# Expert stage of a fused attention and mixture-of-experts layer: hand-overs two pairs of blocks apart, TensorE's steps in reverse order, paired row loads

## The reference

```python
x = x + attention(layernorm(x))              # x: (8, 512, 256)
h = layernorm(x).reshape(4096, 256)
topv, topi = top_k(h @ gate_w.T, 8)          # 8 of 64 experts for each token
rw = softmax(topv)
gate, up = split(einsum('nh,eih->nei', h, gu_w))   # 64 + 64 columns per expert
out = einsum('nei,ehi->nh', silu(gate) * up * W, dp_w)   # W holds rw at topi, else 0
shared = (silu(h @ sh_gate_w.T) * (h @ sh_up_w.T)) @ sh_down_w.T
x = x + out + sigmoid(h @ sh_gate1_w.T) * shared
```

## Time and profile before

| | us |
|---|---|
| median of 3 runs | 1461.35 |
| lowest and highest of them | 1455.36, 1462.63 |
| the profiled execution, its own time | 1475.3 |
| its span from first to last instruction | 1473.5 |
| expert stage: first turn_x to last turn_x | 866.5 to 1425.3 |
| POOL's indirect writes: first to last issue | 876.1 to 1443.2 |
| PE, POOL busy over the whole span | 78%, 50% |

### The profile page before, as it was taken

How to read it: one execution, slowest core, us unless ns; L and a number is a source line. 1 busy time by engine, 2 the same in 40 slices (tenths; PEclk the granted TensorE clock), 3 DMA queues, 4 the chain that set the end, 5 groups by cost and what they waited for, 6 DMA issues and landing times. The chain is left out here.

```text
span 1473.5 us, 26911 instructions
## 1 busy us (share of the span) xinstructions
PE 1155.0 (78%) x7746; PEld 865.3 (59%) x7746; DVE 710.1 (48%) x2210; ACT 665.7 (45%) x1650; POOL 729.7 (50%) x978
## 2 busy tenths in 40 slices
PE   3799989898998989988874048788788888878871
PEld 2566666565665666665543047677677677667650
DVE  2566766566564665655422411111244444444455
ACT  2466555555554455543321024444444445444530
POOL 3101127556374463744556735555555555556541
PEclk9799999999898999988866569999899999999985
DMA  2687757212122121211229655555567777666534
GB/s 77 203 274 239 244 176 249 75 52 91 40 97 71 52 83 47 94 61 64 72 76 325 206 158 157 159 156 160 207 228 259 263 241 261 222 238 219 173 113 153
DMA packets 144735, 233.45 MB, mean 158 GB/s; under 512 B 19831, under 2 KB 122438, under 8 KB 139216
## 3 DMA queue, kind: packets, MB, share of 16 engines
q1 hardware_dynamic: 69776, 101.07, 21.6%
q0 software_dynamic: 27648, 69.28, 13.1%
q10 hardware_dynamic: 47168, 61.35, 12.9%
HBM read 107.32 MB, written 132.66 MB: 163 GB/s over the span
## 5 line engine op out<-in xcount | busy, mean ns | idle before, releaser
L1299 POOL DMA_INDIRECT res_d<-y,dst_i x320 | 319.8, 999 | 261.0 <-ACT y L1151 141.5
L817 DVE TENSOR_REDUCE nmax<-ps 128x1 f32<-128x512 f32 (+3 forms) x448 | 226.2, 532 | 183.2 <-PE ps L474 150.3
L424 POOL DMA_INDIRECT rows_d<-pay,slot_i x256 | 257.4, 1005 | 74.4 <-issue 70.7
L684 ACT ACTIVATE wgu_s<-ps 128x512 f32<-128x512 f32 x320 | 192.0, 601 | 198.9 <-PE ps L515 168.7
L1239 PE MATMUL psB<-wgu_s,xT 128*128 x1280 | 184.0, 290 | 34.2 <-issue 22.7
L472 PE MATMUL ps<-kT,qT 96*128 96x512 f32 (+3 forms) x512 | 198.3, 432 | 9.1 <-DVE nmax L817 6.8
L513 PE MATMUL ps<-qT,kT 128*128 128x512 f32 (+3 forms) x512 | 194.5, 424 | 3.4 <-ACT qT L697 3.2
L1239 PEld LDWEIGHTS psB<-wgu_s,xT 128*128 128x128 f32 x1280 | 166.2, 203 | 43.2 <-issue 42.7
L1066 DVE TENSOR_TENSOR inner<-inner,psB 128x128 f32<-128x128 f32 x160 | 45.6, 285 | 288.4 <-ACT inner L1138 228.4
L1257 PE MATMUL psD<-wdp_s,innerT 128*128 x640 | 178.2, 404 | 0.0
L1131 ACT COPY xT<-psA 128x512 f32<-128x512 f32 x160 | 95.2, 595 | 118.2 <-PE psA L1228 92.0
(11 more groups left out here) (194 smaller groups left out, 1696.5 us busy)
## 6 DMA issues: line engine op xcount, KB each, us to landing
rows_d<-blank ACTq DMA_DIRECT2D x8, 5440.0 KB, 18.9
xg<-rows_d SPq DMA_DIRECT2D x320, 136.0 KB
yk<-res_d SPq DMA_DIRECT2D x32, 1024.0 KB
wgu_s<-wgu_in ACTq DMA_DIRECT2D x8, 1024.0 KB
x_d<-x SPq DMA_DIRECT2D x32, 192.5 KB
xs<-x_d SPq DMA_DIRECT2D x32, 192.5 KB
res_d<-y,dst_i POOLq DMA_INDIRECT x320
wgu_s<-x_in SPq DMA_DIRECT2D x32, 128.0 KB, 2.7
```

The source lines that it names most:

```text
L424: pool.indirect_dma_start(rows_d, bass.IndirectOffsetOnAxis(ap=slot_i[par][:, t, k:k + 1], axis=0), pay[par][:, t, :], None).then_inc(s_sc ...
L684: act.activation(pexp[p % 4][:, s, :], ps2[:, (5 * p + s) % 2, :], ACT.Exp, scale=HEAD_D ** -0.5).then_inc(s_exp, 1)
L817: return dve.tensor_reduce(nmax[u][:, tile, heads[0]:heads[-1] + 1], src, AX.X, ALU.max, negate=True)
L1299: pool.indirect_dma_start(res_d, bass.IndirectOffsetOnAxis(ap=dst_i[:, j % G:j % G + 1], axis=0), y[:, j % Y, :], None, bounds_check=ROUTE ...
```

## The change

**Distances.** PE and ACT now do the four operations of pair i in steps i, i+2, i+4 and i+6 (`GATE`, `TURN`, `DOWN` = 2, 4, 6) and no longer in i to i+3. There are 167 steps instead of 164.

**Order.** Within a step both engines go from the oldest pair to the newest: down(i-6), turn_inner(i-4), gate_up(i-2), turn_x(i). Waits that this order implies are dropped.

**Buffers.** `xT`, `inner`, `innerT` get three buffers (`A`); `psC` gets two banks, and the shared expert uses their free columns instead of `psS`. `dst_i` holds 32 blocks, `y` holds 10 instead of 12.

**Loads.** SP loads two blocks with one DMA (160 of 272 KB) on one semaphore.

**Sums.** All eight additions go to `acc`; `mix` writes `fin` and comes one step after the last addition, in the sixth step of the tile (`MIX` = 5). Because it reads a bank that PE's turn_inner writes in the next step, PE waits there for `mix` (`c_mix`, named shared_added). Sums begin 12 steps after a sequence is complete instead of 9. Five tiles are late instead of four.

```diff
-            G, R, Y = 16, 4, 12
+            G, R, Y, A = 16, 4, 10, 3
+            GATE, TURN, DOWN = 2, 4, 6
-            dst_i = sb("dst_i", [P, G], I32)
+            dst_i = sb("dst_i", [P, 2 * G], I32)
-            psC = ps("psC", [P, SEQ])
-            psS = ps("psS", [P, SEQ])
+            psC = ps("psC", [P, 2, SEQ])
...
-            STEPS = PAIRS + 4
-            LOADED_BEFORE, SUMMED_AFTER, SUM_STEPS = 20, 9, 4
+            STEPS = PAIRS + DOWN + 1
+            LOADED_BEFORE, SUMMED_AFTER = 26, 12
+            SUM_STEPS, TURN_SHARED, DOWN_SHARED, MIX = 4, 2, 4, 5
...
-                    sp.dma_start(xg[:, j % G, :], rows_v[j]).then_inc(e_x[j % G], 16)
+                    sp.dma_start(xg[:, j % G:j % G + 2, :], rows_v[i]).then_inc(e_x[i % (G // 2)], 16)
...
                 def mix(tile):
-                    dve.wait_ge(c_acc[u], TOP * (tile // 2) + TOP - 1)
+                    dve.wait_ge(c_acc[u], TOP * (tile // 2 + 1))
                     dve.wait_ge(c_y_ps, tile + 1)
-                    dve.tensor_tensor(acc[:, u], psS[:, P:P + D], acc[:, u], ALU.add).then_inc(c_mix, 1)
+                    step = STEPS if tile in late_sums else sum_step(tile) + DOWN_SHARED
+                    dve.wait_ge(e_c, min(PAIRS, step - TURN + 1))
...
                 def turn_x(i):
-                    if i >= 2:
-                        pe.wait_ge(e_a, i - 1)
...
                 def gate_up(i):
                     pe.wait_ge(e_a, i + 1)
-                    if i >= 2:
-                        pe.wait_ge(e_in, i - 1)
...
                 def turn_inner(i):
                     pe.wait_ge(e_in, i + 1)
-                    if i >= 1:
-                        pe.wait_ge(e_c, i)
...
                 for i in range(STEPS):
                     if i % 2 == 0 and i < PAIRS:
                         load_offsets(2 * i)
+                    if 0 <= i - DOWN < PAIRS:
+                        down(i - DOWN)
...
+                    for tile, s in tile_at(i - 1):
+                        if s == MIX:
+                            pe.wait_ge(c_mix, tile + 1)
...
+                    if 0 <= i - TURN < PAIRS:
+                        turn_inner(i - TURN)
+                    if 0 <= i - GATE < PAIRS:
+                        gate_up(i - GATE)
                     if i < PAIRS:
                         turn_x(i)
-                    if 0 <= i - 1 < PAIRS:
-                        gate_up(i - 1)
-                    if 0 <= i - 2 < PAIRS:
-                        turn_inner(i - 2)
-                    if 0 <= i - 3 < PAIRS:
-                        down(i - 3)
```

More of the change, by code:

```diff
@@ L963, in build @@
                  "dst_ready shared_tanh shared_gate sh_ready shT_psum shT_ready shared_psum shared_added").split()]
-            e_x = [sem(f"xg_in{k}") for k in range(G)]
+            e_x = [sem(f"xg_in{k}") for k in range(G // 2)]
             e_out = [sem(f"y_out{k}") for k in range(Y)]
@@ L981, in every @@
             def every(tile):
-                return 4 if tile // TILES == BATCH - 2 else 8
+                return 6 if tile // TILES == BATCH - 2 else 8
             def load_turn(tile):
@@ L991, in sum_step @@
                 return (complete(tile) + every(tile) * (tile % TILES)) // 2 + SUMMED_AFTER
-            late_sums = [tile for tile in range(ALL_TILES) if sum_step(tile) + SUM_STEPS >= STEPS]
+            late_sums = [tile for tile in range(ALL_TILES) if sum_step(tile) + MIX >= STEPS]
             def tile_at(step):
                 return [(tile, step - sum_step(tile)) for tile in range(ALL_TILES)
-                        if tile not in late_sums and 0 <= step - sum_step(tile) < SUM_STEPS]
+                        if tile not in late_sums and 0 <= step - sum_step(tile) <= MIX]
+            shared_bank = [(sum_step(tile) if tile not in late_sums else tile) % 2 for tile in range(ALL_TILES)]
             block = ctx.enter_context(nc.Block())
@@ L1016, in _ @@
                 tile = 0
-                for j in range(BLOCKS):
+                for i in range(PAIRS):
+                    j = 2 * i
                     if j >= G:
-                        sp.wait_ge(e_a_ps, (j - G) // 2 + 1)
+                        sp.wait_ge(e_a_ps, i - G // 2 + 1)
                         sp.wait_ge(e_pick, (j - G) // R + 1)
-                    sp.dma_start(xg[:, j % G, :], rows_v[j]).then_inc(e_x[j % G], 16)
-                    while tile < ALL_TILES and load_turn(tile) <= j:
+                    sp.dma_start(xg[:, j % G:j % G + 2, :], rows_v[i]).then_inc(e_x[i % (G // 2)], 16)
+                    while tile < ALL_TILES and load_turn(tile) <= j + 1:
                         load_tile(tile)
@@ L1079, in add @@
                 def add(tile, k):
-                    u, last = tile % 2, k == TOP - 1
+                    u = tile % 2
                     if k == 0:
@@ L1084, in add @@
                         dve.wait_ge(c_acc[u], TOP * (tile // 2) + k)
[L1085 to L1088, removed]
                     at = tile * TOP + k
-                    dve.scalar_tensor_tensor(out=(fin if last else acc)[:, u], in0=yk[:, u, k],
-                                             scalar=rw_all[:, at:at + 1],
+                    dve.scalar_tensor_tensor(out=acc[:, u], in0=yk[:, u, k], scalar=rw_all[:, at:at + 1],
                                              in1=xs[:, u, 0:D] if k == 0 else acc[:, u],
@@ L1118, in _ @@
                     for k in range(TOP):
-                        if k == TOP - 1:
-                            mix(tile)
                         add(tile, k)
+                    mix(tile)
             @block.scalar
@@ L1184, in _ @@
                             shared(tile)
-                        if s == 1:
-                            shT_copy(tile)
-                    while stored not in late_sums and sum_step(stored) + SUM_STEPS <= i:
+                    while stored not in late_sums and sum_step(stored) + MIX < i:
                         store(stored)
@@ L1262, in turn_shared @@
                     pe.wait_ge(c_sh, tile + 1)
-                    if tile >= 1:
-                        pe.wait_ge(c_mix, tile)
-                    pe.transpose(psS[0:INNER, 0:P], sh[:, tile % 2, :], ident).then_inc(c_t_ps, 1)
+                    pe.transpose(psC[0:INNER, shared_bank[tile], 2 * P:3 * P], sh[:, tile % 2, :], ident).then_inc(c_t_ps, 1)
                 def down_shared(tile):
                     pe.wait_ge(c_t, tile + 1)
-                    pe.matmul(psS[:, P:P + D], shT[:, tile % 2, :], shd_w[0:INNER, :], start=True, stop=True).then_inc(c_y_ps, 1)
+                    pe.matmul(psC[:, shared_bank[tile], 2 * P:2 * P + D], shT[:, tile % 2, :], shd_w[0:INNER, :],
+                              start=True, stop=True).then_inc(c_y_ps, 1)
                 for i in range(STEPS):
```

102 lines of the change are left out of this document (57 added, 45 removed).

## The result

The changed kernel takes 1440.05 us (median of 4 runs, 1437.32 to 1443.55), the kernel before 1461.99 us in the runs beside it (median of 4). The ratio is 0.986, 95% interval 0.983 to 0.989. The forecast was 1407 us, its own range 1380 to 1439, the whole range 1340 to 1468. The result lies 1 us above the forecast's own range, at its border with rival B (1468 us, gains down to 1440).

The account below looks back on a forecast made before the run. No engine is full; POOL starves in 62 long gaps, 152 us together, behind late PE releases. Fewer gaps -61 us, later first y +7, net -54 from 1461.35: 1407 us, own range 1380 to 1439, whole range 1340 to 1468.

Parts of the forecast that it names:

- rival B: POOL's long gaps stay, extra margin buys nothing, only fill counts: 1468 us, gains down to 1440; chance 17%.
- What bounds the kernel: Expert stage: no engine is full; POOL works in bursts, then starves in 62 long gaps, 152.4 us, 2.46 us each.
- Growth of the delay: ACT learns of PE's work later the longer POOL's burst lasts: about 0.65 us per us, up to 4.9 us.
- rival A: POOL's long gaps go altogether: -120 us, 1341 us; chance 18% with what lies between (1335 to 1380).
- Margins: How late ACT's copy may be before PE stalls: 1.7 us before, 2.8 us after the change.
- Burst length: POOL's pairs between long gaps: 2.6 before; after, 5 in 59 steps without sums, 4 in 101 with sums.
- the term for the stock in the chain: Three added pairs between turn_x and y come out once late releases arrive: 0 to 7.7 us of POOL's work.
- Rival C: PE's wait for mix costs one long gap in each of 27 tiles: +46 us net, 1507 us; chance 15%.
- The sum: POOL's long gaps after the change: 37 at 2.46 us, 91 us against 152, so -61 us.
- Fill: First y comes three steps of 2.41 us later, before POOL can start: +7 us.
- End: Fifth late tile, 5 us of DVE and gate after the last steps, hidden by the late load: 0, or +5.
- Loads and ring: Paired loads on SP and the ring of 32 destinations on DVE: 0 us each.

Follow-up runs that it names:

- g1: Changed kernel as it is, on a chip without late releases: 1287.5 us, 0.991 of the kernel before.
- e4: Changed kernel with three more PE releases a pair, on a semaphore nobody waits for; chip without late releases: 1286.9 us, 0.991 of the kernel before.
- j2: Changed kernel with distances 1, 2, 3; POOL writes 80 pairs, then SP writes y by plain DMAs; chip with late releases: 1418.9 us.
- g2: Changed kernel without PE's shared-expert work and every wait for mix; chip without late releases: 1287.1 us, 0.990 of the kernel before.
- k1: Changed kernel with mix moved ahead of gated on DVE; chip with late releases: 1449.4 us, 0.984 of the kernel before.
- i1: Kernel before with only paired loads and the ring of 32 destinations; chip without late releases: 1293.1 us, 0.996 of the kernel before.
- f1: Changed kernel again as it is, on a chip with late releases: 1441.3 us, 0.986 of the kernel before.

## Why the prediction was right in its direction and wrong in its size

**What bounds the kernel: right.** Long gaps of POOL, 2.4 to 2.5 us each in all kernels on late chips, fed by releases of PE that come later the longer POOL runs. With the gaps gone by themselves (g1) POOL's run is 418 us, and the kernel 1287.5 us.

**Growth of the delay: right.** About 0.65 us per us was read from one cycle of the kernel before, 0.70 from one of the changed kernel. It goes on growing up to 5.7 us, where rival A wanted no growth once nothing is blocked. A falls. Whether it grows with time or with the number of releases is open (e4).

**Margins: right in kind.** By the prediction's own formula distance one in reversed order leaves down + turn_inner less the copy, 0.87 + 0.21 - 0.7 = 0.4 us. That delay is reached 1.8 us into a burst, plus 2.9 us: 4.7 us, 1.8 pairs. j2 has 2.2. The kernel before with 1.7 us has 2.7, the changed one with 2.8 us was to have at least 3.3 and has 3.3 to 3.6 in three profiles where no sums run.

**Burst length: the step that failed, in both its terms.** The prediction divided 59 steps by 5 pairs and 101 by 4, which is 12 and 25 long gaps; 15 and 37 were found. So 3 of the missing gaps belong to the steps without sums and 12 to those with them.

*Without sums* 5 pairs was "the middle" between none and all of the chain's three added pairs coming out as y. The measured 3.3 to 3.6 lie next to none: the term for the stock in the chain should have been near nothing. Why is not shown. The cycle allows two readings. From 924.67 to 927.84 ACT stands at silu of pair 21, whose release is missing, and behind it in ACT's fixed order stand xT of pair 23 and the y copy of pair 18. By the first reading the late release holds the older pair behind it, and ACT can't reach the stock. But ACT then waits another 1.18 us for xT of pair 23, which PE had made ahead of pair 18's down product. If the releases arrive in PE's order, that y copy had nothing to take until 929.29, and an ACT that could pass silu would gain nothing. No run tells the two apart.

*With sums* 4 pairs were taken, on the grounds that the wait for mix sets the distance between stops. It is 204 / 2 / 37 = 2.8 pairs, from 106 / 45 = 2.4. POOL starves more often than once a tile, so something other than that wait ends its bursts, and they were shorter with sums in the kernel before too, where the prediction took 2.6 throughout. What shortens them wasn't found; g2 might have shown it on a late chip. Rival C's mechanism is there (16 to 17 waits of PE for fin), but it adds no gaps: they fell here too, by 8. k1 took away six of the waits and gained nothing.

**The sum.** Gaps: 37 forecast, 52 and 51 found; -33 and -16 us in the two pairs of profiles, against -61. In the first pair POOL's run is 30.4 us shorter, it waits 1.7 us longer for its first write, and from its end to the span's end it is 0.4 us less: the 29 us from the first turn_x on. Had the lower bound been taken (3.3 pairs everywhere, 48 gaps, -34), the net would have been -27, within 5 us of the measured -22, in part by luck, as the fill in it is 5 us too high.

**Fill: too high.** +7 was forecast. POOL waits 14.46 us for its first write and not 12.72:

```profile
872.28 1.00 POOL L1308 DMA_INDIRECT res_d<-y,dst_i  x1 [14.46 <-ACT y L1157]
```

That is +1.7 us. The steps of the fill are not 2.41 us long, since most of their operations aren't there yet. Turn_x stands at 866.21, 867.76 and 869.31:

```profile
866.21 0.60 PE L1233 MATMUL psA<-cst,xg 128*128 128x128 f32 x4
...
867.76 0.60 PE L1233 MATMUL psA<-cst,xg 128*128 128x128 f32 x4
...
869.31 0.60 PE L1233 MATMUL psA<-cst,xg 128*128 128x128 f32 x4
```

1.55 us a step.

**End: right.** From the last write's end to the span's end it was 29.3 us and is 28.9. The fifth late tile is hidden: DVE is through with one tile at 1411.08, and what comes next waits for a load until 1415.50, ACT for 8.08 us:

```profile
1410.66 0.42 DVE L1104 TENSOR_TENSOR fin<-psC,acc 128x256 f32<-128x256 f32 x1
...
1415.50 0.26 ACT L1164 ACTIVATE act_s<-xs 128x64 f32<-128x64 f32 x1 [8.08 <-DMA xs<-x_d]
```

**Loads and ring: not nothing.** 0 was forecast. On a prompt chip they give 5 us (i1). For late chips it wasn't measured; there the waits for destinations fell from 23.6 us in 9 to 14.2 in 7.

**Rival B** named the size better than its reason: distance does count (j2), but by the estimate above more than half of what it gives is spent on the rest of the change.

## To carry to other kernels

More distance between engines lengthens a run by the room that it gives a late item; pairs that merely stand in the chain behind late releases gave next to nothing here, so leave them out of the sum until a row shows one coming out. When distance comes together with another order and other buffers, price each alone: here the rest cost some 25 us of the 41 that the distance gave. And before tuning around a late hand-over, see what else is active while it is late: with POOL silent the same stage ran at 2.70 us a pair instead of 3.6, which no distance came near.

## What was not expected of the hardware

The same program takes 1460 to 1473 us on some chips and 1298 to 1299 on others, each run within 1% of its chip's median, with the granted clock nearly alike in the profiled executions (0.886 of the kernel before on a late chip, 0.904 of the changed one on a prompt chip). The difference is in the time from a product's end to its release: 0.03 us in the cycle shown of a prompt chip, up to 5.7 us in that of a late one while POOL issues indirect DMAs one after the other, and 0.03 us there too once POOL is silent. It is not confined to this stage: the attention stage, where POOL scatters rows, has it in f1, on its line L817 (the first three lines are the expert stage's).

```profile
ACT inner L1144 <- remote: 60.9, 31, 3.9
ACT xT L1137 <- remote: 37.7, 37, 2.6
ACT y L1157 <- remote: 27.7, 20, 2.3
DVE nmax L817 <- remote: 20.8, 9, 4.6
```

On prompt chips no wait at all is put to "<-remote". Hand-overs from ACT to DVE were prompt in every cycle shown (silu to gated, 0.03 us). What sets a chip's kind stays open.
